# Row maxima of the attention scores split before the transpose instead of after it

## What is computed

```python
theta = jnp.einsum('bhwc,cd->bhwd', x, W_theta)
phi = _maxpool2x2(jnp.einsum('bhwc,cd->bhwd', x, W_phi))
g = _maxpool2x2(jnp.einsum('bhwc,cd->bhwd', x, W_g))
...
beta = jax.nn.softmax(jnp.einsum('bqd,bkd->bqk', theta, phi), axis=-1)
tmp = jnp.einsum('bqk,bkv->bqv', beta, g).reshape(B, H, W, Cc // 2)
o = jnp.einsum('bhwv,vc->bhwc', tmp, W_o)
return gamma * o + x
```

## Time and profile before

| | |
|---|---|
| median of 3 runs | 245.92 us (245.24 to 248.23) |
| the profiled execution, its own time | 245.17 us |
| its span from first to last instruction | 243.3 us |
| outside the span | 1.9 us |
| granted TensorE clock | 1.000, all slices at 9 tenths or more |
| PE busy | 234.0 us (96%), 1464 matmuls |
| DVE busy | 207.0 us (85%) |
| ACT busy | 147.5 us (61%) |
| POOL busy | 167.4 us (69%) |

### The profile page before, as it was taken

The page is one execution under the profiler, slowest core; times in us unless marked ns, Lnnn a source line. Parts: engine busy times, 40 slices in busy tenths (PEclk is TensorE's granted clock), DMA queues, the critical chain, the costliest instruction groups (busy, mean ns, idle before and its releaser), DMA issues.

```text
span 243.3 us, 4331 instructions
## 1 busy us (share of the span) xinstructions
PE 234.0 (96%) x1464; PEld 208.6 (86%) x1464; DVE 207.0 (85%) x474; ACT 147.5 (61%) x274; POOL 167.4 (69%) x119
## 2 busy tenths in 40 slices
PE   6988989999999999999999999999999999998994
PEld 4676888998989899898989989898998989897894
DVE  5896978979989897988989799898979889898775
ACT  3854947758474774947467494746749375644550
POOL 1766696876779587677958767795876769542680
PEclk9999999999999999999999999999999999999999
DMA  6790019368392946839195682929568292807644
GB/s 236 275 382 34 0 57 345 125 176 343 104 338 82 325 195 173 348 94 352 75 314 205 164 359 96 334 92 312 206 221 297 71 343 114 306 40 266 253 175 178
DMA packets 14934, 51.14 MB, mean 210 GB/s; under 512 B 1856, under 2 KB 2496, under 8 KB 14912
## 3 DMA queue, kind: packets, MB, share of 16 engines
q1 hardware_dynamic: 14512, 50.67, 58.6%
q10 hardware_dynamic: 400, 0.20, 0.3%
HBM read 33.95 MB, written 16.78 MB: 208 GB/s over the span
## 4 chain that ended last, share of the span: by engine, by line
PE 82%; DVE 6%; ACT 4%; POOL 2%; DMA 2%; issue 2%; ACTq 1%; SPq 0%; DVEq 0%
PE proj L207 31%; PE out L324 25%; PE shift L324 10%; PE shift L295 6%; PE score L244 6%; PE score L271 4%; DMA x_t<-in_xt 2%; DVE neg_parts L606 1%; DVE out L581 1%; POOL e_lo L534 1%; POOL x_lo L529 1%; DVE g_max L599 1%; DVE y_sb L632 1%; DMA theta<-neg_lo 1%; PE proj L200 1%
## 5 line engine op out<-in xcount | busy, mean ns | idle before, releaser
L534 POOL TENSOR_TENSOR e_lo<-e_sb,e_hi 128x512 fp32r<-128x512 f32 x64 | 81.9, 1292 | 51.7 <-ACT e_sb L461 51.7
L529 POOL TENSOR_TENSOR x_lo<-x_t,x_hi 128x1024 fp32r<-128x1024 f32 x30 | 71.8, 2396 | 6.8 <-ACT x_hi L418 6.8
L324 PE MATMUL out<-G_hi,e_hi 128*128 128x258 f32 x184 | 52.4, 285 | 0.3 <-DVE y_sb L632 0.2
L324 PE MATMUL out<-G_lo,e_hi 128*128 128x258 f32 x184 | 52.1, 283 | 0.0
L324 PE MATMUL out<-G_hi,e_lo 128*128 128x258 f32 x184 | 52.0, 282 | 0.0
L632 DVE SCALAR_TENSOR_TENSOR y_sb<-out,r_sum,x_n 128x256 f32<-128x256 f32 x92 | 44.5, 484 | 6.7 <-DVE r_sum L623 0.5
L207 PE MATMUL proj<-x_hi,w_hi 128*128 128x512 f32 x122 | 48.4, 397 | 1.7 <-DVE g_max L599 1.0
L207 PE MATMUL proj<-x_hi,w_lo 128*128 128x512 f32 x122 | 48.3, 396 | 0.0
L207 PE MATMUL proj<-x_lo,w_hi 128*128 128x512 f32 x122 | 48.2, 395 | 0.0
L606 DVE TENSOR_REDUCE neg_parts<-score 128x2 f32<-128x512 f32 x64 | 43.5, 685 | 1.1 <-PE score L244 0.2
L458 ACT ACTIVATE e_hi<-shift 128x512 fp32r<-128x512 f32 x60 | 36.0, 600 | 11.2 <-PE shift L295 10.4
(11 more groups left out here) (91 smaller groups left out, 396.3 us busy)
## 6 DMA issues: line engine op xcount, KB each, us to landing
x_t<-in_xt SPq DMA_DIRECT2D x32, 512.0 KB, 5.1
x_n<-in_xn SPq DMA_DIRECT2D x32, 512.0 KB, 7.0
out<-y_sb SPq DMA_DIRECT2D x31, 512.0 KB, 6.2
w_sb<-in_w_proj SPq DMA_DIRECT2D x1, 256.0 KB, 2.7
theta<-neg_hi ACTq DMA_DIRECT2D x16, 4.0 KB
theta<-neg_lo SPq DMA_DIRECT2D x16, 4.0 KB
out<-y_sb SPq DMA_DIRECT2D x1, 256.0 KB, 2.5
wo_sb<-in_w_out SPq DMA_DIRECT2D x1, 128.5 KB, 5.0
```

The costliest lines, as they stand in the source:

```text
L324: last = nc.tensor.matmul(out_bank(i, t)[:, 0:GW], e[:, i % 2, KC * h + k, cells], G[:, i % 3, k, :], start=(n == 0), stop=(n == 3 * KC - 1))
L529: nc.gpsimd.tensor_tensor(x_lo[:, i % 2, h], x_t[:, i % 2, h], x_hi[:, i % 2, h].bitcast(f32), ALU.subtract).then_inc(x_lo_ready, 1)
L534: nc.gpsimd.tensor_tensor(e_lo[:, i % 2, n, :], e_sb[:, n, :], e_hi[:, i % 2, n, :].bitcast(f32), ALU.subtract).then_inc(e_lo_ready, 1)
```

## The change

DVE splits the 128x8 maxima while they are still columns: `split_maxima` makes a rounded copy in columns 0 to 7 of `neg_split` and the remainder in columns 8 to 15. One transpose then turns both, ACT copies 16 rows in one instruction (`neg_round`), and both row DMAs start from that copy: ACT's queue sends rows 0 to 7, SP's queue rows 8 to 15. `neg_low` is gone from DVE. `split_maxima(b)` comes right behind `maxima(b, 3)`, ahead of the finishes. The transpose now also waits for the split and stands inside an output, after its third matmul: output 3 of image d in the loop, `output(13, 2)` for image 14 and `output(14, 0)` for image 15.

```diff
-        neg_parts = sb("neg_parts", [P, P])
-        neg_hi, neg_lo = sb("neg_hi", [TILES, P], f32r), sb("neg_lo", [TILES, P], f32r)
+        neg_parts = sb("neg_parts", [P, TILES])
+        neg_split, neg_rows = sb("neg_split", [P, P]), sb("neg_rows", [2 * TILES, P], f32r)
...
             def max_into_stack(i):
-                sp.wait_ge(neg_lo_ready, i + 1)
-                sp.dma_start(max_row(i, 1), neg_lo[:, :].bitcast(f32)).then_inc(neg_in[i % 3], 16)
+                sp.wait_ge(neg_rows_ready, i + 1)
+                sp.dma_start(max_row(i, 1), neg_rows[TILES:2 * TILES, :].bitcast(f32)).then_inc(neg_in[i % 3], 16)
...
                 pe.wait_ge(max_ready, 4 * i + 4)
-                nc.tensor.transpose(neg_bank[:, 0:P], neg_parts[:, :], ident[:, :]).then_inc(neg_turned, 1)
+                pe.wait_ge(neg_lo_ready, i + 1)
+                nc.tensor.transpose(neg_bank[:, 0:P], neg_split[:, :], ident[:, :]).then_inc(neg_turned, 1)
...
+                        if n == 3 and turn is not None:
+                            turn_max(turn)
                 last.then_inc(out_ready, 1)
...
                     outputs(d, (0, 1, 2))
-                    turn_max(b)
-                    outputs(d, (3, 4))
+                    output(d, 3, turn=b)
+                    output(d, 4)
...
             shifted(LAST - 1, 3)
-            turn_max(LAST)
-            outputs(LAST - 1, (0, 1, 2, 3))
+            output(LAST - 1, 0, turn=LAST)
+            outputs(LAST - 1, (1, 2, 3))
...
-            def neg_high(i):
+            def neg_round(i):
                 act.wait_ge(neg_turned, i + 1)
                 if i > 0:
                     act.wait_ge(neg_in[(i - 1) % 3], neg_loads(i - 1))
-                nc.scalar.copy(neg_hi[:, :], neg_bank[0:TILES, 0:P]).then_inc(neg_hi_ready, 1)
-                act.wait_ge(neg_hi_ready, i + 1)
-                act.dma_start(max_row(i, 0), neg_hi[:, :].bitcast(f32)).then_inc(neg_in[i % 3], 16)
+                nc.scalar.copy(neg_rows[:, :], neg_bank[0:2 * TILES, 0:P]).then_inc(neg_rows_ready, 1)
+                act.wait_ge(neg_rows_ready, i + 1)
+                act.dma_start(max_row(i, 0), neg_rows[0:TILES, :].bitcast(f32)).then_inc(neg_in[i % 3], 16)
...
-            def neg_low(i):
+            def split_maxima(i):
+                dve.wait_ge(max_ready, 4 * i + 4)
+                if i > 0:
+                    dve.wait_ge(neg_turned, i)
+                v.tensor_copy(neg_split[:, 0:TILES].bitcast(f32r), neg_parts[:, 0:TILES]).then_inc(neg_hi_ready, 1)
                 dve.wait_ge(neg_hi_ready, i + 1)
-                if i > 0:
-                    dve.wait_ge(neg_in[(i - 1) % 3], neg_loads(i - 1))
-                v.tensor_tensor(neg_lo[:, :], neg_bank[0:TILES, 0:P], neg_hi[:, :].bitcast(f32),
+                v.tensor_tensor(neg_split[:, TILES:2 * TILES], neg_parts[:, 0:TILES], neg_split[:, 0:TILES],
                                 ALU.subtract).then_inc(neg_lo_ready, 1)
...
                     maxima(b, 3)
+                    split_maxima(b)
                 if a < LAST:
                     finishes(d, (0, 1))
-                    neg_low(b)
                     finishes(d, (2, 3, 4, 5))
```

More of the change, by code:

```diff
@@ L105, in nonlocal_block @@
         score_ready, max_ready = sem("score_ready"), sem("max_ready")
-        neg_hi_ready, neg_lo_ready = sem("neg_hi_ready"), sem("neg_lo_ready")
+        neg_hi_ready, neg_lo_ready, neg_rows_ready = sem("neg_hi_ready"), sem("neg_lo_ready"), sem("neg_rows_ready")
         neg_turned = sem("neg_turned")
@@ L238, in scores @@
                     if i > 0:
-                        pe.wait_ge(neg_lo_ready, i)
+                        pe.wait_ge(neg_rows_ready, i)
                 else:
@@ L283, in shifted @@
                     elif n == 1:
-                        pe.wait_ge(neg_lo_ready, i + 1)
+                        pe.wait_ge(neg_rows_ready, i + 1)
                     elif n == 2:
@@ L297, in shifted, with output @@
                                  start=True, stop=True).then_inc(shifted_ready, 1)
-            def output(i, t):
+            def output(i, t, turn=None):
                 h, w = divmod(t, HT)
@@ L387, in _ @@
             outputs(LAST - 2, (0, 1))
-            turn_max(LAST - 1)
             scores(LAST, 0)
-            outputs(LAST - 2, (2, 3))
+            output(LAST - 2, 2, turn=LAST - 1)
+            output(LAST - 2, 3)
             scores(LAST, 1)
@@ L476, in _ @@
             x_high(2, 1)
-            neg_high(0)
+            neg_round(0)
             phi_high(1)
@@ L501, in _ @@
                     g_high(a)
-                neg_high(b)
+                neg_round(b)
                 if a < LAST:
@@ L507, in _ @@
             exps(LAST - 1, 2)
-            neg_high(LAST)
+            neg_round(LAST)
             exps(LAST - 1, 3)
@@ L604, in maxima @@
                 if n == 0 and i > 0:
-                    dve.wait_ge(neg_turned, i)
+                    dve.wait_ge(neg_lo_ready, i)
                 v.tensor_reduce(neg_parts[:, 2 * n:2 * n + 2], score[n % 2][:, :].rearrange("p (t k) -> p t k", t=2),
                                 AX.X, ALU.max, negate=True).then_inc(max_ready, 1)
-            def neg_low(i):
+            def split_maxima(i):
[3 more added lines that the diff above has]
+                v.tensor_copy(neg_split[:, 0:TILES].bitcast(f32r), neg_parts[:, 0:TILES]).then_inc(neg_hi_ready, 1)
                 dve.wait_ge(neg_hi_ready, i + 1)
-                if i > 0:
-                    dve.wait_ge(neg_in[(i - 1) % 3], neg_loads(i - 1))
-                v.tensor_tensor(neg_lo[:, :], neg_bank[0:TILES, 0:P], neg_hi[:, :].bitcast(f32),
+                v.tensor_tensor(neg_split[:, TILES:2 * TILES], neg_parts[:, 0:TILES], neg_split[:, 0:TILES],
                                 ALU.subtract).then_inc(neg_lo_ready, 1)
@@ L633, in finish @@
                                        x_n[:, i % 2, h, w, :], ALU.mult, ALU.add).then_inc(y_ready, 1)
-            v.memset(neg_parts[:, :], 0.0).then_inc(fixed_ready, 1)
+            v.memset(neg_split[:, :], 0.0).then_inc(fixed_ready, 1)
             v.memset(phi[THETA:STACK, :, :].bitcast(f32), 1.0).then_inc(fixed_ready, 1)
@@ L671, in _ @@
             maxima(0, 3)
+            split_maxima(0)
             phi_pool(1, 1)
             theta_low(1, 1)
-            neg_low(0)
             phi_low(1)
@@ L691, in _ @@
             maxima(1, 3)
+            split_maxima(1)
             for s in range(2, B):
@@ L711, in _ @@
             finishes(LAST - 2, (0,))
-            neg_low(LAST - 1)
             maxima(LAST, 0)
@@ L718, in _ @@
             maxima(LAST, 3)
+            split_maxima(LAST)
             finishes(LAST - 2, (6,))
-            neg_low(LAST)
             finishes(LAST - 2, (7,))
```

## The result

The changed kernel takes 263.85 us (median of 4 runs, 263.48 to 264.65), the kernel before 246.32 beside it (4 runs, 245.24 to 248.23): 1.0707 times as long, interval 1.0633 to 1.0780. The forecast was 246.7 with a range up to 248.8, so it was wrong by 17 us. The profiled execution takes 263.58 with a span of 261.8, 18.5 more than before.

What follows compares the result with a forecast made beforehand. TensorE was taken as the bound. Terms -2.0 (row wait) + 1.9 (output 4) + 0.2 (start) + 1.2 (end) = +1.3 us on 245.17 gave 246.5; 0.2 added for run scatter made 246.7 us, range up to 248.8.

Steps and rivals of the forecast that it cites:

- Moved: DVE's split ahead of the first finish: VectorE, each loop body: split takes 0.405 us against 0.23 us spare, delaying output 4; cost 1.9 us.
- the four rivals: Short split 244.3 us (0.2); row DMAs colliding 250.9 (0.08); end absorbs delay 245.4 (0.12); nothing seen 246.6.
- The remainder row's wait: Before `shifted(b, 0)`: row DMA issued 0.29 us earlier ends the wait; gain 11 x 0.14 + 0.42 = 2.0 us.
- The two row DMAs: Rival: issued together, one waits for the other's issue, 0.37 us lost in each of twelve bodies; 250.9 us, chance 0.08.
- Output 4 late by 0.17 us: Output 4's weight load waits for the first finish, pushed by the split, in eleven bodies; cost 1.9 us.
- just in time: Moved transpose: split reaches PE at 104.74, its weight load would start at 104.78, so no added wait.
- The start: Image 0: split before a projection's pooling delays the transpose; 0 to 0.41 us, taken as 0.2.
- The end: Last transpose, behind three matmuls of `output(14, 0)`, delays `exps(14, 3)` and `mix(15)`; cost 1.2 us, bounds 0.1 to 1.4.
- Short split: Rival: both small operations take 0.07 us, split 0.21 us, output 4 costs nothing; 244.3 us, chance 0.2.

Runs made afterwards that it cites:

- the second execution of the reductions: Changed kernel with both split operations as reductions of one SBUF input, run once more beside the one with the last transpose put back: 247.34 us (12 runs).
- the pair of runs above: Kernel with both reductions, last transpose put back ahead of `output(14, 0)`, against the same kernel without that: 246.89 and 247.34 us (12 runs each).

## Why the prediction was wrong, point by point

**The step that failed** is "Moved: DVE's split ahead of the first finish", and in it the two durations, 0.16 and 0.175 us. The arithmetic on them was right: alone they take 0.172 and 0.168. But the rows they came from the earlier trace rows are from the first microseconds, when GpSimd was not yet at work on `x_low`, and the sum used them in a place where GpSimd is in the middle of `x_low`. The bounds (0.21 to 0.5 us for the whole split) were drawn from sizes of operations; none asked what runs beside them. The split took 1.16 us in a body and 3.9 at image 0, and none of the four rivals contained it.

The trace of before could not have shown it in the loop. Every VectorE operation there has at most one tensor from SBUF (the finishes take a column of scalars besides), the others from PSUM. The change brought in the loop's first two operations that stay in SBUF, and that this was new in kind was in the diff.

The start of that trace had a sign, though, with the roles reversed. GpSimd's remainder of W_o has the shape of `g_low` (0.73 us), but begins while VectorE makes an `x_lo` from two SBUF inputs, and takes 1.14:

```profile
7.97 1.21 DVE L658 TENSOR_TENSOR x_lo<-x_t,x_hi 128x1024 fp32r<-128x1024 f32 x1
8.64 1.14 POOL L545 TENSOR_TENSOR wo_lo<-w_og,wo_hi 128x256 fp32r<-128x256 f32 x1 [0.52 <-ACT wo_hi L467]
```

It ends 0.60 us behind VectorE's end at 9.18. In eight other kernels of this study it begins 0.39 to 0.76 us before VectorE's end in the same way; there it takes 0.98 to 1.35 us and ends 0.58 to 0.60 behind that end. In the three traces with both reductions it begins 0.12 us before that end or later, and takes 0.74.

The Trainium skill states the rule, and the prediction, which weighed another page of it, missed it. "SBUF — State Buffer", section "Who interferes with whom", says that a VectorE instruction with two SBUF inputs contends with a GpSimd instruction that reads SBUF, that fp32 copies and casts within SBUF can too, that one with at most one SBUF input outside those modes doesn't, and that the later one waits for the whole of the earlier. The runs agree with each: 0.65 and 2.26 us for the subtraction, 0.45 for the copy, 0.16 to 0.17 for the reductions.

**The remainder row's wait** (2.0 us gained): right in its mechanism, with a gain of 1.4 us where it was measured alone. The pair is at 0.47 in the changed kernel as predicted. In the kernel with `neg_low` earlier, the eleven distances between transposes from image 2 to 13 sum to 1.4 us less than before, and the measured gain is 0.56% or 1.4 us. That kernel still has bodies of 14.15, where 14.23 less 0.14 makes 14.09; what takes the rest is open.

**The two row DMAs** (rival, 250.9): out as a cost of every body. SP and ACT issue at 101.20 and 101.21 in body s = 6, and the load of the shifted matmul, 2.12 us behind, doesn't wait. With inputs from PSUM it doesn't wait in ten of the twelve bodies, at 2.07 to 2.09 us, which is just where the rival would begin; in the other two it comes at 2.15, and about 0.1 us is lost. So the margin is thin, and in one body each the load waits longer for a row DMA, 0.16 us in the changed kernel, 0.27 with the reductions, and 1.14 in the second execution of the reductions (issue at 63.29, load at 66.59):

```profile
66.59 0.30 PEld L297 LDWEIGHTS shift<-theta,phi 98*128 98x128 f32 x2 [1.14 <-DMA theta<-neg_rows]
```

Whether the two rows held each other up there, no run shows.

**Output 4 late by 0.17 us** (1.9 us lost): right with the durations that it assumed. In the kernel with inputs from PSUM its weight load starts 0.27 us behind the one before it, instead of 0.12, so 0.15 late; and the bodies stay at 14.23, as in the sum, where the gain on the row and the loss at output 4 nearly cancel.

```profile
106.23 0.19 PEld L325 LDWEIGHTS shift<-G_hi,e_lo 128*128 128x128 f32 x1
...
106.50 0.19 PEld L325 LDWEIGHTS out<-G_hi,e_hi 128*128 128x128 f32 x1
```

In the changed kernel the loss came mostly as a wait of the transpose itself, 0.66 us beyond the usual distance of 0.12 between matmuls, which the prediction held to be "just in time".

**The start** (0.2): 6.5 us in the changed kernel. Two splits beside whole `x_low`s cost 3.5 and 2.6 us more than assumed. The term was too small even without waits for GpSimd: with inputs from PSUM and with the reductions, the first distance between transposes is 14.92 to 14.98 us in all four traces, against 14.32 before, and in the first traces of the two kernels the transpose of image 1 starts at 34.02 and 34.10 us instead of 32.60. So the start cost 0.6 us at least, for a reason that stays open, and the agreement of those kernels with 246.7 is partly luck.

**The end** (1.2): right. From `shifted(14, 3)` to `mix(15)` it is 6.07 us with the reductions and 4.86 before, 1.21 more; 0.95 of it is the move by the pair of runs above. In the changed kernel the last split took 0.56 and 1.18 us beside `e_low`s, 1.4 us more than assumed. With the term of 1.2 that makes 2.6 us, against 2.4 measured.

**Short split** (rival, 244.3, by the memset's 0.07): out; the operations never took less than 0.16.

## What to carry to other kernels

A duration taken from a trace holds for what ran beside it there: before a VectorE operation is moved or added, look at GpSimd's timeline at the new place, and count its SBUF inputs. An operation that waits for GpSimd costs up to the longest instruction there (2.3 us here), whatever its own size. If it must stand there, make it a reduction of one SBUF input, let it read PSUM, or put it where GpSimd idles; on a path with no slack the wait is paid in full.

## What had not been expected

- A copy of 128x8 between SBUF tensors waits for GpSimd (0.45 us), while a reduction that does the same work on the same tensors does not (0.161 us, all sixteen times).
- The wait is for the instruction that is running, not for GpSimd to be idle. `x_low` and `g_low` overlap by 0.04 us in the records (97.33 + 2.40 against 99.69), and the copy ends at 99.76 although `g_low` has started.
- GpSimd loses nothing in the loop: `x_low` takes 2390 ns on average in the changed kernel, 2403 in the kernel of the reductions, where VectorE never waits for it.
- Behind the stall that VectorE's 8 elements caused at image 1, TensorE's granted clock was 0.74 over 6.5 us, where the kernel before has 1.00.
